# Layer 1 attention: values after the projection, rows of maxima by ACT's queue, packs loaded together, dummy matmuls

## The reference

```
def _L1_attn_ref(x, W_q, W_k, W_v, W_o, W_down_kv, W_up_k, W_up_v):
    q = x @ W_q
    k = x @ W_k
    v = x @ W_v
    latent_kv = (k + v) @ W_down_kv
    k_rec = (latent_kv @ W_up_k).reshape(b, s, H, HD).transpose(0, 2, 1, 3)
    v_rec = (latent_kv @ W_up_v).reshape(b, s, H, HD).transpose(0, 2, 1, 3)
    ...
    scores = jnp.einsum('bhqd,bhkd->bhqk', qh, k_rec) / math.sqrt(d)
    scores = scores * decay[None, None, :, :]
    attn = jax.nn.softmax(scores, axis=-1)
    out = jnp.einsum('bhqk,bhkd->bhqd', attn, v_rec)
    out = out.transpose(0, 2, 1, 3).reshape(b, s, d)
    return out @ W_o
```

## Time and profile before

| | us |
|---|---|
| runs of the kernel before, median of 3 | 1570.79 |
| lowest, highest | 1562.11, 1572.23 |
| the profiled execution | 1561.7 |
| its span in the trace | 1559.6 |

### The profile page before, as it was taken

The page is one execution under the profiler, slowest core; times in us unless marked ns, Lnnn a source line. Parts: engine busy times, 40 slices in busy tenths (PEclk is TensorE's granted clock), DMA queues, the critical chain, the costliest instruction groups (busy, mean ns, idle before and its releaser), DMA issues. The chain is left out here.

```text
span 1559.6 us, 23543 instructions
## 1 busy us (share of the span) xinstructions
PE 1334.3 (86%) x7952; PEld 751.4 (48%) x7952; DVE 1128.4 (72%) x1737; ACT 906.1 (58%) x1496; POOL 474.1 (30%) x986
## 2 busy tenths in 40 slices
PE   4298988619999999999754989999999979999998
PEld 1133333407877778777321222222222225777776
DVE  4366674377999999998547766888888243778885
ACT  3288885105555555555330766787887802767774
POOL 3255453003343343343220233223442301212210
PEclk8599999859999999999855898999999968999999
DMA  5524420015666666663347556665563040022110
GB/s 139 107 56 88 80 61 8 3 41 127 151 150 147 151 155 140 157 148 72 123 96 92 72 128 123 102 106 87 88 98 49 15 157 3 26 97 82 61 49 27
DMA packets 71415, 142.57 MB, mean 91 GB/s; under 512 B 11815, under 2 KB 44648, under 8 KB 64392
## 3 DMA queue, kind: packets, MB, share of 16 engines
q1 hardware_dynamic: 70660, 140.62, 41.3%
q10 hardware_dynamic: 648, 0.59, 0.1%
HBM read 124.20 MB, written 16.71 MB: 90 GB/s over the span
## 5 line engine op out<-in xcount | busy, mean ns | idle before, releaser
L1385 DVE CUSTOM_DVE_ANT_0 a_junk<-a_mring,a_COR 128x1024 bf16<-128x1024 f32 x256 | 304.8, 1222 | 90.0 <-PE a_mring L1286 89.8
L1373 ACT ACTIVATE a_PR<-a_ring 128x512 f32<-128x512 f32 x576 | 300.7, 603 | 118.7 <-PE a_ring L1317 118.6
L1260 POOL TENSOR_SCALAR_AFFINE_SELECT a_PR<-a_PR 128x128 f32<-128x128 f32 x512 | 134.6, 293 | 304.0 <-ACT a_PR L1373 303.8
L803 ACT ACTIVATE e_HH<-e_H 128x512 fp32r<-128x512 f32 x184 | 116.4, 633 | 162.5 <-DVE e_H L851 161.8
L1317 PE MATMUL a_ring<-a_QP,a_KP 74*128 74x512 bf16 (+3 forms) x768 | 181.2, 341 | 13.1 <-issue 5.7
L402 DVE TENSOR_SCALAR a_PR<-a_PR,a_lo,a_hi 128x1024 f32<-128x1024 f32 (+1 forms) x160 | 122.1, 774 | 77.1 <-ACT a_PR L376 74.4
L376 ACT ACTIVATE a_PR<-a_ring,a_ng 128x1024 f32<-128x1024 f32 (+1 forms) x160 | 155.0, 1033 | 13.3 <-PE a_ring L305 12.5
L1336 PE MATMUL a_OUT<-a_PR,a_V 128*9 128x512 f32 (+3 forms) x1536 | 154.7, 500 | 0.0
L822 DVE TENSOR_TENSOR e_HL<-e_H,e_HH 128x512 fp32r<-128x512 f32 x138 | 140.3, 1017 | 13.2
L1317 PEld LDWEIGHTS a_ring<-a_QP,a_KP 74*128 74x128 bf16 x768 | 57.9, 99 | 172.4 <-ACT a_PR L1373 119.6
L1676 DVE TENSOR_TENSOR e_HL<-e_GL,e_HH 128x512 fp32r<-128x512 f32 x144 | 109.2, 763 | 37.6 <-ACT e_HH L1644 34.1
(11 more groups left out here) (232 smaller groups left out, 2344.8 us busy)
## 6 DMA issues: line engine op xcount, KB each, us to landing
e_ROUTE<-routing SPq DMA_DIRECT2D x24, 704.0 KB
a_QP<-q_parts SPq DMA_DIRECT2D x72, 192.0 KB
e_RAW<-in_w_chunks SPq DMA_DIRECT2D x46, 192.0 KB, 7.5
a_QM<-q_parts SPq DMA_DIRECT2D x64, 128.0 KB, 5.4
e_GATE<-gates SPq DMA_DIRECT2D x8, 1024.0 KB, 4.7
e_ROUTE<-routing SPq DMA_DIRECT2D x8, 640.0 KB
a_KP<-k_parts SPq DMA_DIRECT2D x24, 192.0 KB
e_ROUTE<-routing SPq DMA_DIRECT2D x8, 576.0 KB
```

The lines of the kernel that those rows point to most:

```text
L803: nc.scalar.activation(HH[n % NH][:], HT[n % NH][:], ACT.Copy).then_inc(high_done, 1)
L1260: last = nc.gpsimd.affine_select(out=d, in_=d, compare_op=keep, fill=0.0, base=0, pattern=[[step, P]], channel_multiplier=-step)
L1373: nc.scalar.activation(PR[g % NPR][:, j, :], ring[n % NRING][:], ACT.Exp).then_inc(s_read, 1)
L1385: nc.vector.tensor_tensor_reduce(out=junk[:, i % 2, :], in0=mring[k % 2][:], in1=COR[:, c:c + S], scale=1.0, scalar=-3.0e38, op0=ALU.mult, ...
```

## The change

- The values leave the projection. The latent tile `lat` now outlives it. In the attention block PE makes all 16 value matmuls first, three to a bank of the score ring, and ACT copies them to V in six copies.
- ACT issues the first key max pack after all its work of the projection.
- After each of the 22 first maxima PE issues three matmuls whose result nothing reads (`keep_busy`), and 12 more before the first score. The wait for OUT's clearing moves behind them.
- `max_rows` moves from SP's program to ACT's: for half 0 ahead of the first exponential, for the others one group after the turn.
- SP issues the key and the query pack together in even halves, and both packs of quad 1 right after the first loads. The late stores are issued 12 at a time, in halves 1 and 3.
- The stores of the output have a semaphore for each parity.

Its core:

```diff
@@ -919,17 +916,7 @@
                         pe.wait_ge(val_done, (g - 2) * NV + 2)
                     nc.tensor.matmul(psQ[g % 2][:], W["wq"][:], xg, start=True, stop=True).then_inc(q_ready, 1)
 
-                def values(f):
-
-                    if f:
-                        pe.wait_ge(v_kept, f)
-                    for n in range(FILL):
-                        at = (f * FILL + n) * P
-                        last = nc.tensor.matmul(psV[:, n * VW:(n + 1) * VW], lat[:, at:at + P], WV[:], start=True, stop=True)
-                    last.then_inc(v_ready, 1)
...
@@ -984,17 +965,11 @@
                     first_part(g, 3)
                     second_part(g, 2)
                     second_part(g, 3)
-                    if g == NG - 2:
-                        act.wait_ge(first_stored, 2 * NV * 2 * 16)
-                        mp.load_k(act, 0)
+                act.wait_ge(first_stored, 2 * NV * 2 * 16)
+                mp.load_k(act, 0)
 
             @block.vector
             def _(dve):
...
                                                     ALU.subtract).then_inc(rest_done, 1)
-                            if g and w % 2 == 0:
-                                keep_values((g - 1) * PAIR_FILLS + w // 2 - 1)
                 for w in range(1, NV, 2):
                     third_part(NG - 1, w)
-                    keep_values((NG - 1) * PAIR_FILLS + w // 2)
 
...
             def _(sp):
-                def max_rows(h):
-
-                    s = h // 2 % 2
-                    sp.wait_ge(m_read, turn_slots[h] + 1)
-                    for i in range(2):
-                        sp.dma_start(QP[s][PAIRS + i:PAIRS + i + 1, h % 2].rearrange("p j a t -> p (j a t)"), MT[:, i, :]).then_inc(m_rows, 16)
-
                 def store(h):
 
                     sp.wait_ge(out_read, h + 1)
-                    sp.dma_start(OD[h // 2, :, h % 2 * GW:(h % 2 + 1) * GW], OST[h % 2][:]).then_inc(out_stored, 16)
+                    sp.dma_start(OD[h // 2, :, h % 2 * GW:(h % 2 + 1) * GW], OST[h % 2][:]).then_inc(out_stored[h % 2], 16)
 
                 def store_late(n):
 
...
                 mp.load_q(sp, 1)
-                max_rows(0)
                 mp.load_k(sp, 1)
-                max_rows(1)
                 for h in range(NHALF):
                     it = h // 2
                     if h:
                         store(h - 1)
-                    if it + 1 < NIT:
-                        if h % 2 == 0:
+                    if h % 2 == 0:
+                        if it + 1 < NIT:
                             if it >= 1:
                                 sp.wait_ge(s_read, it * 2 * UNITS)
+                            load_pack_k(sp, it + 1)
                             load_pack_q(sp, it + 1)
-                        if h % 2 == (it >= 1):
-                            load_pack_k(sp, it + 1)
-                    if 0 < h < NHALF - 1:
-                        max_rows(h + 1)
-                    if 1 <= h <= 3:
-                        for n in range((h - 1) * LATE_STORES // 3, h * LATE_STORES // 3):
+                        if it + 2 < NIT:
+                            sp.wait_ge(m_read, tile_slot((h + 2) * NTILE - 1) + 1)
+                            if it + 2 == NQUAD:
+                                sp.wait_ge(stored[1], LATE_STORES * 16)
+                            mp.load_q(sp, it + 2)
+                            mp.load_k(sp, it + 2)
+                    elif h <= 3:
+                        for n in range(h // 2 * (LATE_STORES // 2), (h // 2 + 1) * (LATE_STORES // 2)):
                             store_late(n)
-                    if h % 2 == 0 and it + 2 < NIT:
-                        sp.wait_ge(m_read, tile_slot((h + 2) * NTILE - 1) + 1)
-                        if it + 2 == NQUAD:
-                            sp.wait_ge(stored[1], LATE_STORES * 16)
-                        mp.load_q(sp, it + 2)
-                        mp.load_k(sp, it + 2)
                 store(NHALF - 1)
-                sp.wait_ge(out_stored, NHALF * 16)
+                for half in range(2):
+                    sp.wait_ge(out_stored[half], NIT * 16)
...
 
+                def values(f):
+
+                    if f >= NRING:
+                        pe.wait_ge(v_kept, f - NRING + 1)
+                    for n in range(f * FILL, min(f * FILL + FILL, B * KB)):
+                        last = nc.tensor.matmul(ring[f % NRING][:, n % FILL * VW:(n % FILL + 1) * VW], lat[:, n * P:(n + 1) * P], WV[:],
+                                                start=True, stop=True)
+                    last.then_inc(v_ready, 1)
+
+                def keep_busy(n):
+
+                    nc.tensor.matmul(ring[n % NRING][:], mp.K[0][:, 0, 0, 0:P], mp.Q[0][:, 0, 0, 0:GW], start=True, stop=True)
+
+                for f in range(NFILL):
+                    values(f)
                 pe.wait_ge(ones_loaded, 32)
                 pe.wait_ge(cor_loaded, 32)
-                pe.wait_ge(out_clear, 1)
                 for m in range(LEAD):
                     if m == tiles_until_turn(0):
                         turn(0)
                     max_tile(m)
+                    if m == 0:
+                        pe.wait_ge(v_kept, NFILL)
+                    for n in range(3):
+                        keep_busy(n)
+                for n in range(12):
+                    keep_busy(n)
+                pe.wait_ge(out_clear, 1)
                 for g in range(NGROUP + LAG):
                     if g < NGROUP:
                         for j in range(HQ - 1):
@@ -1359,12 +1347,31 @@
 
                     act.wait_ge(pv_done, (h + 1) * NT)
                     if h >= 2:
-                        act.wait_ge(out_stored, (h - 1) * 16)
+                        act.wait_ge(out_stored[h % 2], h // 2 * 16)
                     nc.scalar.activation(OST[h % 2][:], OUT[:], ACT.Copy).then_inc(out_read, 1)
+
+                def max_rows(h):
+
+                    s = h // 2 % 2
+                    act.wait_ge(m_read, turn_slots[h] + 1)
+                    for i in range(2):
+                        act.dma_start(QP[s][PAIRS + i:PAIRS + i + 1, h % 2].rearrange("p j a t -> p (j a t)"), MT[:, i, :]).then_inc(m_rows, 16)
+
+                def keep_values(f):
+
+                    n = min(FILL, B * KB - f * FILL)
+                    act.wait_ge(v_ready, f + 1)
+                    nc.scalar.activation(V[:, f * FILL:f * FILL + n].rearrange("p n c -> p (n c)"), ring[f % NRING][:, 0:n * VW], ACT.Copy).then_inc(v_kept, 1)
 
                 for s in range(2):
                     act.dma_start(KP[s][PAIRS:PAIRS + 2].rearrange("p j a t -> p (j a t)"), ones16).then_inc(ones_loaded, 16)
+                for f in range(NFILL):
+                    keep_values(f)
+                max_rows(0)
                 for g in range(NGROUP):
+                    for h in range(1, NHALF):
+                        if turn_group(h) + 1 == g:
+                            max_rows(h)
                     for j in range(HQ):
                         n = g * HQ + j
                         act.wait_ge(s_filled, n + 1)
```

More of the change, by code:

```diff
@@ L873, in project_l1 @@
         psQ, psKV, psK = ([pb(f"p1_{n}{s}") for s in range(2)] for n in ("psQ", "psKV", "psK"))
[L874 to L876 removed]
+        psL = pb("p1_psL")
+        q_ready, kv_ready, kv_read, lat_ready, lat_read, k_ready, val_done, rest_done, part1, part2, part3, ones_set = (
+            sem(f"p1_{n}") for n in ("q_ready", "kv_ready", "kv_read", "lat_ready", "lat_read", "k_ready",
                                      "val_done", "rest_done", "part1", "part2", "part3", "ones_set"))
@@ L1117, in attention_l1 @@
     LATE_STORES = 4 * NPART * 2
+    FILL = GW // VW
+    NFILL = -(-B * KB // FILL)
     def issued(g):
@@ L1157, in attention_l1 @@
         PR = [sb(f"a1_PR{r}", [P, HQ, GW], F32) for r in range(NPR)]
-        COR, ID, V, late, stored = (t[n] for n in ("COR", "ID", "V", "late", "stored"))
+        COR, ID, V, late, stored, lat, WV = (t[n] for n in ("COR", "ID", "V", "late", "stored", "lat", "WV"))
         junk = sb("a1_junk", [P, 2, S], BF16)
@@ L1168, in attention_l1 @@
         cor_loaded = t["cor_loaded"]
-        ones_loaded, out_clear, s_filled, s_read, m_filled, m_read, masked, pv_done, out_read, out_stored, neg_done, m_rows = (
-            sem(n) for n in ("ones_loaded", "out_clear", "s_filled", "s_read", "m_filled", "m_read", "masked", "pv_done", "out_read", "out_stored",
+        v_ready, v_kept = sem("v_ready"), sem("v_kept")
+        out_stored = [sem(f"out_stored{half}") for half in range(2)]
+        ones_loaded, out_clear, s_filled, s_read, m_filled, m_read, masked, pv_done, out_read, neg_done, m_rows = (
+            sem(n) for n in ("ones_loaded", "out_clear", "s_filled", "s_read", "m_filled", "m_read", "masked", "pv_done", "out_read",
                              "neg_done", "m_rows"))
```

22 lines of the change are left out of this document (4 added, 18 removed).

## The result

| | before | after |
|---|---|---|
| median of 4 runs, us | 1566.81 | 1622.15 |
| lowest, highest | 1562.11, 1572.23 | 1613.35, 1626.83 |
| ratio, 95% interval | | 1.0345 (1.0284 to 1.0407) |

The changed kernel is 3.5% slower; the forecast was 1548 us, faster. What happened is the first rival, which had a chance of 0.1 and a price of 1607, with the late start of the second rival on top of it.

A forecast was written before the change was run, and what follows sets the result against it. TensorE was taken to bound the steady attention, with chains of waits around layer 1's start. Terms -15.3 + 6 - 5.5 - 14.5 + 3 + 5 = -21.3 us gave 1540 from the profiled 1561.7; 1548 was taken, range 1528 to 1576.

The forecast's parts named there:

- first rival: Odd halves: rows land 11.5 us after issue, about 9 us lost each, +37 us in all, 1607; chance 0.1.
- second rival: Attention start: dummies at low clock and half 0's rows meeting two quads' packs, +15, give the gain back, 1562; chance 0.2.
- Rows against packs: Odd halves: each row DMA waits for one pack DMA, 0.7 us in each of seven halves, +5 us.
- the 11.5 us of the ones: Before the first maximum: the ones' landing beside full queues in the old trace, 826.47 - 814.95, cited for the first rival.
- the 6.0 that I had worked out: Odd halves: second row DMA lands at most 1.9 + 4.1 = 6.0 us after issue, 1.3 too late.
- Low clock in half 0: First score to first output copy: a clock raised beforehand saves time there, -5.5 us, bounds -6 and -2.
- Dummies, +6: First maximum to first score: the added dummy matmuls cost 3 us plus 3 us, bounds +3 to +12.
- Projection, -15.3: Layer 1's projection block: gaps, copies and loads removed or moved end it near 799 instead of 814 us, -15.3 us.
- Two stalls: Output copies, stalls of 7.4 and 6.3 us plus 0.8: new issue order removes them, -14.5 us, bounds -14.5 and 0.
- ACT as issuer: Steady attention: 15 pairs of row DMAs issued between exponentials cost 0.2 us each, +3 us, bounds 0 and 18.
- The values at nothing in the shadow of the ones: Before the first maximum: value matmuls, 10.6 us, fit in the 12.2 us wait for the ones and cost nothing.

The follow-up runs named there:

- a_old_queue: Changed kernel with the rows of maxima back on SP's queue and SP's old order of loads, values and dummies kept: 1565.44 us, ratio 0.997.
- f_no_dummies: Changed kernel without the dummy matmuls: 1613.3 us, ratio 1.0257.
- g_reordered: a_old_queue with SP's loads reordered (even halves query pack, rows, key pack; odd halves max pack, rows; half 0's rows before quad 1's packs): 1545.56 us, ratio 0.9847.
- h_act_held: g_reordered with ACT issuing the rows and SP holding its next load back until they have landed: 1544.68 us, ratio 0.9854.
- e_no_packs: Changed kernel with the pack loads of quads 2 to 7 left out, so it computes with old ones: 1558.48 us in one run.
- b_key_odd: Changed kernel with only the key pack moved back to the odd half: 1577.0 us, ratio 1.0035.
- k_packs_alone: Changed kernel with the next max pack moved from the even to the odd half: 1597.52 us, ratio 1.0196.

## Why the prediction was wrong

- **The step that failed: "Rows against packs", +5 us.** It said that each row DMA waits for one pack DMA, lands at most 1.3 us late, and costs 0.7 us in each of seven odd halves. Measured: PE waits 2.9 to 9.65 us for them in all seven, 53.2 us with half 0's wait, and the six halves after half 1 cost 61.3 us. Most packets of the rows waited not for one pack DMA but for nearly all that SP had issued ahead. The first rival's 9 us per half (63 us) was the right size, and the 11.5 us of the ones beside full queues were the right size of a landing (the row DMAs took 9.6 to 15.0 in these six halves). I gave it 0.1 because the ones are two rows only; the rows of maxima, in 32 pieces, did no better (13.6 us from issue to PE's score in half 5). Two things were left out of the sum: the next max pack, issued at 991.63 us into the same stretch (with it the waits go from 24.7 to 49.5 us), and the clock that falls after each stall (46.6 us of waits, 61.3 of time).
- **Two rules of one section of the Trainium skill** ("DMA: Bandwidth & Descriptors", Queues, rings and completion order). I used the one that a DMA engine takes turns between queue rows a packet at a time, and worked it into a delay of a few pack requests. The traces do not agree with that size: 72 packets of the rows stood for 8 us in half 5 while 900 of the other queue went through; and the 11.5 us of the ones, which I called agreement, are nearly twice the 6.0 that I had worked out. A few lines on, the section says that a DMA's semaphore increment is a strongly ordered write, which lands only after every earlier write of that DMA engine, "across its queues". That is about the signal and not about the start of a packet, and it isn't what held the rows here: in half 5 the last of their packets ran at 1006.9 us, and the DMA landed 0.9 us later.
- **"Low clock in half 0", -5.5 us: nothing came.** The clock rose before the scores and fell within 5 us of them (a_old_queue: score to copy 34.5 against 33.2). In the changed kernel the stretch grew by 8.4 us; the 2.91 us wait for the rows of half 1 lies in it, and no run splits the rest.
- **Dummies, +6: right in size** (5 in a_old_queue), but the stretch to the first score took 11.6 longer. The second rival's row was right: the rows of half 0 met quad 1's packs (12 us), and f_no_dummies has 34.4 us there without a dummy. It said +15 and is wrong only in that it was no rival but a part of the same mechanism.
- **Projection, -15.3: right** (-15.2), for the reasons given; the block's end at 40 us and the wait for the ones (11.9 us) came as foretold.
- **Two stalls, -14.5: right** as a mechanism, 13.6 in g_reordered. The changed kernel had this gain too.
- **ACT as issuer, +3: right**, 2.4 by h_act_held. The values at nothing in the shadow of the ones: right.

The measured stretches add up to -15.2 - 0.3 + 11.6 + 8.4 + 49.5 = +54.0 us where -21.3 was forecast; and the 49.5 between the first and the last copy are the 61.3 of the six stalls, less the 14.5 of the old ones, and 2.6 of small delays before the halves 2, 6 and 10.

**What stays open.** Why the packets of one queue wait on a DMA engine until those of the other have gone: the runs show that they do, not what orders them. In e_no_packs and b_key_odd more had moved than was issued ahead, by 0.5 to 0.7 MB, so "all that was issued ahead" is not the whole of it there. Nor do the runs show why layer 1 starts up to 10 us earlier or later from one execution to another.

## What to carry to other kernels

Before two loads are issued together to start one of them earlier, count every small DMA with a deadline that falls into their time, and price it at all the bytes then issued and not landed, divided by the measured rate, whichever queue it uses. Keep such a DMA clear by the order of the large ones (behind one that will have landed, ahead of the next), and add the low clock to each wait of TensorE that this leaves. Read from the windows after the first one whether the clock that dummy matmuls have raised is kept; here it was not, and they cost 5 us or more.

## What the runs showed of the hardware

- 16 KB in two DMAs on ACT's queue took 1.8 us each to land alone, 11.5 to 15.0 beside two packs and a max pack on SP's queue, and 8.6 to 9.9 where the max pack came half a turn later (k_packs_alone, halves 3 to 13).
- A second queue let only 24 of the 96 packets of these rows through at once; 72 stood for 5 to 11 us until the other queue's loads were nearly done (changed kernel, k_packs_alone, f_no_dummies, 18 halves).
- Six query-pack DMAs, of 24 partitions each, had 72 packets of 4 bytes, 12 each, against 16 for a row DMA or an output store (b_key_odd).
- SP was itself held while issuing: six query-pack DMAs took 2.66 us in g_reordered, 4.80 in half 5 of the changed kernel and 12.76 at its start; eight of the max pack 3.71 and 8.92. In all of these a long span of a DMA issue in the timeline stood where the loads were behind.
- TensorE's granted clock fell from 1.00 to 0.50 while PE went from 4.09 to 5.00 busy of 5 us, in the first groups of scores, with the DMAs idle; in the steady halves, at 48.16 of 50 us, it stays at 1.00.
